# The second mix placed directly behind the first on two other PSUM banks, in a fused convolution and feed-forward block

## The reference, cut to what matters

```python
x = x + conv(layernorm_over_channels(x))
t = tokens(x)                                  # (4, 16384, 48)
t = t + ffn(layernorm_over_channels(t))
return from_tokens(t)

# conv: 3x3 convolution of the first 12 channels, the others pass by
#       1x1 convolution 48 -> 254 channels                          ("mix")
#       in each 8x8 patch: irfft2(rfft2(patch) * fft_w)             ("weigh", "inverse")
#       a, b = halves of 127 channels;  gelu(a) * b                 ("gelu", "gate")
#       1x1 convolution 127 -> 48                                   ("project")
# ffn:  h = relu(quantised(q_mul(x) @ q_mul(W1).T + q_mul(b1)))      48 -> 192
#       y =      quantised(q_mul(h) @ q_mul(W2).T + q_mul(b2))       192 -> 48
```

## Time and profile before

| | |
|---|---|
| median of 3 runs (lowest, highest) | 719.0 us (718.56, 719.1) |
| the profiled execution | 720.83 us |
| its span, first to last instruction | 718.9 us |
| busy share PE, PEld, DVE, ACT, POOL | 93%, 73%, 84%, 75%, 67% |
| mean granted TensorE clock | 0.983 |

### The profile page before, as it was taken

How to read it: one execution, slowest core, us unless ns; L and a number is a source line. 1 busy time by engine, 2 the same in 40 slices (tenths; PEclk the granted TensorE clock), 3 DMA queues, 4 the chain that set the end, 5 groups by cost and what they waited for, 6 DMA issues and landing times.

```text
span 718.9 us, 19183 instructions
## 1 busy us (share of the span) xinstructions
PE 670.5 (93%) x6699; PEld 521.3 (73%) x6699; DVE 600.7 (84%) x1141; ACT 541.3 (75%) x1077; POOL 480.8 (67%) x354
## 2 busy tenths in 40 slices
PE   1579999999999999999999999999999999999973
PEld 1467788777777887778777877778777877777741
DVE  5436789888889898998999999888899899977785
ACT  3144578878888888888888888888888887777774
POOL 2752667877767777877777778777777778753351
PEclk9989999999999999999999999999999999999995
DMA  3342332333434432343334333434433324331111
GB/s 76 90 101 69 85 83 68 88 102 85 106 90 105 103 92 70 100 95 96 101 97 106 98 80 80 106 91 100 94 103 105 102 55 100 87 99 43 29 30 53
DMA packets 46486, 62.22 MB, mean 87 GB/s; under 512 B 19039, under 2 KB 34871, under 8 KB 46391
## 3 DMA queue, kind: packets, MB, share of 16 engines
q1 hardware_dynamic: 45143, 60.91, 33.7%
q10 hardware_dynamic: 1248, 0.08, 0.1%
HBM read 44.62 MB, written 16.35 MB: 85 GB/s over the span
## 4 chain that ended last, share of the span: by engine, by line
PE 76%; DVE 8%; POOL 7%; issue 3%; DMA 2%; ACTq 1%; ACT 1%; SPq 1%; DVEq 0%; POOLq 0%
PE inva L474 15%; PE mixp L461 14%; PE invb L481 14%; PE misc L673 7%; PE misc L490 5%; POOL st L1262 5%; PE misc L545 4%; PE misc L511 4%; PE misc L606 3%; PE misc L658 3%; PE misc L596 2%; PE misc L520 2%; DVE st L1176 2%; DVE qpix L1066 1%; PE misc L568 1%
## 5 line engine op out<-in xcount | busy, mean ns | idle before, releaser
L1009 DVE TENSOR_TENSOR gmix<-mixp,freq_w 128x508 f32<-128x508 f32 x256 | 162.9, 677 | 10.1 <-PE mixp L461 10.1
L474 PE MATMUL inva<-inv,gmix 128*127 128x128 f32 x1024 | 138.8, 279 | 0.2 <-DVE gmix L1009 0.2
L481 PE MATMUL invb<-inv,gmix 128*127 128x128 f32 x1024 | 135.5, 275 | 0.1
L474 PEld LDWEIGHTS inva<-inv,gmix 128*127 128x127 f32 x1024 | 127.0, 192 | 8.6 <-issue 7.8
L461 PE MATMUL mixp<-win,zh 60*128 60x254 f16 x1024 | 120.9, 273 | 5.2 <-DVE gmix L1009 3.5
L481 PEld LDWEIGHTS invb<-inv,gmix 128*127 128x127 f32 x1024 | 124.6, 192 | 0.7 <-DVE hbuf L1020 0.3
L461 PE MATMUL mixp<-win,zl 60*128 60x254 f16 x1024 | 119.6, 269 | 0.0
L1262 POOL TENSOR_TENSOR st<-st,neg_half 128x16 f32<-128x16 f32 x32 | 92.8, 2901 | 36.1 <-DVE st L1185 36.1
L759 ACT ACTIVATE hid<-misc 128x512 f16<-128x512 f32 x186 | 100.9, 599 | 18.2 <-PE misc L545 18.2
L1295 POOL TENSOR_TENSOR st<-st,neg_half 128x16 f32<-128x16 f32 x32 | 98.6, 3080 | 16.8 <-DVE st L1092 16.8
L745 ACT ACTIVATE gact<-inva 127x512 f32<-127x512 f32 x128 | 76.9, 601 | 36.2 <-PE inva L474 36.2
(11 more groups left out here) (122 smaller groups left out, 1223.2 us busy)
## 6 DMA issues: line engine op xcount, KB each, us to landing
xin<-in_x_dram SPq DMA_DIRECT2D x64, 192.0 KB, 3.4
xres<-in_x_dram SPq DMA_DIRECT2D x64, 192.0 KB, 4.2
out_dram<-ob SPq DMA_DIRECT2D x62, 192.0 KB, 2.7
taps<-cz_scratch SPq DMA_DIRECT2D x32, 292.5 KB
crm<-rm_scratch SPq DMA_DIRECT2D x64, 96.0 KB
cz_scratch<-cz SPq DMA_DIRECT2D x64, 48.8 KB
cx<-in_x_dram SPq DMA_DIRECT2D x32, 96.0 KB
rm_scratch<-rm_t SPq DMA_DIRECT2D x120, 4.0 KB
```

The lines of the kernel that those rows point to most:

```text
L474: mm = pe.matmul(inva[0:HID, q * PX:(q + 1) * PX], gmix[:, s % 2, q, 0:HID], inv[:], start=True, stop=True, skip_group_check=True)
L481: mm = pe.matmul(invb[0:HID, q * PX:(q + 1) * PX], gmix[:, s % 2, q, HID:HID2], inv[:], start=True, stop=True, skip_group_check=True)
L1009: dve.tensor_tensor(gmix[:, s % 2, 2 * q:2 * q + 2, 0:HID2], mixp[q][:, 0:2 * HID2].rearrange("p (e c) -> p e c", e=2), freq_w[:], ALU.mul ...
```

## The change

`mix(t, 1)` now writes to `bank[1]` and `bank[2]` and stands directly behind `mix(t, 0)` on PE, ahead of the projection. The projection's second half goes to `bank[0]`, as `bank[2]` is taken, and the second layer uses the `mixp` pair, which weigh 0 must have read. On DVE `weigh(t, 1)` moves from behind `scale_tokens` to directly behind `weigh(t, 0)`, ahead of the two residual additions. Waits are added or exchanged where a bank has a new user. The number of instructions stays the same on each engine, and the order on ACT, POOL and SP is unchanged.

```diff
             def mix(t, s):
-                pe.wait_ge(gmix_ready, upto(8 * n + 2 * s))
+                pe.wait_ge(gmix_ready, upto(8 * n + 2 * (s if s != 1 else 0)))
+                pair = (bank[1], bank[2]) if s == 1 else mixp
...
             def second_layer(t):
-                    pe.wait_ge(xsq_ready, upto(2 * a + 2, 2 * STEPS))
-                    pe.wait_ge(lo_ready, upto(2 * n + 2, 2 * STEPS))
+                pair = mixp
+                pe.wait_ge(gmix_ready, upto(8 * n + 2, 8 * STEPS))
+                pe.wait_ge(y16_ready, upto(2 * l))
...
             def turn_tokens(t):
                 pe.wait_ge(qpix_ready, upto(k + 1))
+                pe.wait_ge(tch_ready, upto(2 * m + 2, 2 * STEPS))
+                pe.wait_ge(gmix_ready, upto(8 * n + 4, 8 * STEPS))
...
-                    pe.wait_ge(y16_ready, upto(2 * l + 2))
...
             def turn_rest(t):
                 pe.wait_ge(tch_ready, upto(2 * m + 2))
+                pe.wait_ge(gmix_ready, upto(8 * n + 4, 8 * STEPS))
...
                     mix(t, 0)
+                    pe.wait_ge(xsq_ready, upto(2 * a + 2, 2 * STEPS))
+                    pe.wait_ge(hid16_ready, upto(6 * l + 6))
+                    mix(t, 1)
                 if live(t, 4):
-                    pe.wait_ge(lo_ready, upto(2 * n + 1, 2 * STEPS))
+                    pe.wait_ge(lo_ready, upto(2 * n + 2, 2 * STEPS))
                     project(t, 0, bank[3])
-                    pe.wait_ge(hid16_ready, upto(6 * l + 6))
-                    project(t, 1, bank[2])
+                    project(t, 1, bank[0])
...
                 if live(t, 3):
-                    mix(t, 1)
                     inverse(t, 3, 0)
...
                 if live(t, 3):
+                    pe.wait_ge(y16_ready, upto(2 * l + 2))
                     mix(t, 2)
...
             def residual(t, half):
-                dve.tensor_tensor(split(dst), split(bank[(3, 2)[half]][:]),
+                dve.tensor_tensor(split(dst), split(bank[(3, 0)[half]][:]),
...
                 if live(t, 3):
                     weigh(t, 0)
+                    weigh(t, 1)
                 if live(t, 4):
                     residual(t, 0)
                     residual(t, 1)
...
                     scale_tokens(t)
-                if live(t, 3):
-                    weigh(t, 1)
```

More of the change, by code:

```diff
@@ L460, in mix @@
                             r0 = HALF * q
-                            mm = pe.matmul(mixp[q][:, e * HID2:(e + 1) * HID2],
+                            mm = pe.matmul(pair[q][:, e * HID2:(e + 1) * HID2],
                                            zpart[r0:r0 + KC, 2 * s + e, :], win[r0:r0 + KC, wpart, :],
@@ L548, in second_layer @@
             def second_layer(t):
[L550 to L556, removed]
-                    pe.wait_ge(xsq_ready, upto(2 * a + 2, 2 * STEPS))
-                    pe.wait_ge(lo_ready, upto(2 * n + 2, 2 * STEPS))
+                n, l = at(t, 3), at(t, 6)
+                pair = mixp
+                pe.wait_ge(gmix_ready, upto(8 * n + 2, 8 * STEPS))
+                pe.wait_ge(y16_ready, upto(2 * l))
                 if late(t, 6):
@@ L582, in turn_tokens @@
             def turn_tokens(t):
-                a, n, k, l = (at(t, d) for d in (0, 3, 5, 6))
+                a, n, m, k, l = (at(t, d) for d in (0, 3, 4, 5, 6))
                 peeled = not FIRST <= t[1] < LAST
                 pe.wait_ge(qpix_ready, upto(k + 1))
+                pe.wait_ge(tch_ready, upto(2 * m + 2, 2 * STEPS))
+                pe.wait_ge(gmix_ready, upto(8 * n + 4, 8 * STEPS))
                 pe.wait_ge(lo_ready, upto(2 * n + 2, 2 * STEPS))
@@ L591, in turn_tokens @@
                     pe.wait_ge(hid16_ready, 6 * LATE + (2 if k > LATE else 0))
-                else:
-                    pe.wait_ge(y16_ready, upto(2 * l + 2))
                 pe.sem_inc(pe_held, 1)
@@ L601, in turn_rest @@
             def turn_rest(t):
-                m = at(t, 4)
+                n, m = at(t, 3), at(t, 4)
                 pe.wait_ge(tch_ready, upto(2 * m + 2))
+                pe.wait_ge(gmix_ready, upto(8 * n + 4, 8 * STEPS))
                 for i in range(PAIRS):
@@ L840, in sums @@
             def sums(t, halves_of):
-                a, l = at(t, 0), at(t, 6)
-                pair = mixp if isinstance(a, int) and a >= TOTAL - 3 else (bank[1], bank[0])
+                l = at(t, 6)
+                pair = mixp
                 act.wait_ge(out_ready, upto(l))
@@ L1009, in weigh @@
                     dve.tensor_tensor(gmix[:, s % 2, 2 * q:2 * q + 2, 0:HID2],
-                                      mixp[q][:, 0:2 * HID2].rearrange("p (e c) -> p e c", e=2),
+                                      pair[q][:, 0:2 * HID2].rearrange("p (e c) -> p e c", e=2),
                                       freq_w[:], ALU.mult).then_inc(gmix_ready, 1)
```

## The result

The changed kernel takes 741.9 us (median of 4 runs, 741.6 to 743.6) against 718.8 us for the kernel before on the same chip: a ratio of 1.033, 95% interval 1.0313 to 1.0346. It is slower by 23 us. The profiled execution has a span of 739.6 us, 20.7 more than before. The difference is less than 23 because the profiled execution of the kernel before, 720.83, was 2 us above its median.

A forecast was written before the change was run, and what follows sets the result against it. PE's work and DVE's chain up to `qpix` were taken to bound the kernel together. 27 x 2.43 = 65.6, minus 6.3, minus 1, gave +58.3 us: 779.1 on the profiled execution, forecast 777, range 744 to 785.

The forecast's parts named there:

- The bound: PE's own work and DVE's chain up to `qpix` end within 0.05 us; delaying `qpix` is paid every step.
- Mix 1 ahead of the projection: On PE, the same matmuls in another order: gain and loss nil in undisturbed steps.
- Weigh 1: On DVE, 1.19 us ahead of `rm`, less 0.79 cover: with DVE alone the step loses 0.40 us.
- `xcen` first by 0.09: POOL's `xcen` starts at 275.25, 0.09 ahead of DVE's `rm` at 275.34, and shuts DVE out.
- POOL doesn't let go between `xcen` and `zpix`: `rm` is shut out until `zpix` ends, so `qpix` starts 2.43 us later in each of 27 steps.
- two signs: The prediction is wrong if `rm` lasts 0.17, or `turn_tokens` starts other than 1.1 behind `qpix`.
- POOL lets both through: Rival: `rm` and `qpix` both run behind `xcen`, 1.32 us a step, net +28, 747; chance 0.10.
- The long steps: Lengthenings from POOL's `cz` work: all 6.3 us given back, bounds 0 and 6.3; the bias meets no `zpix`.
- Steps 3 and 4: Steps without `turn_tokens`, where mix 1's wait partly falls away: 1 us gained for both, bounds 0 and 2.
- the clock falls: Rival: PE's clock drops in its new gap of some 2.4 us a step, +67, 845; chance 0.04.

The follow-up runs named there:

- taking the chain away: Kernel before with only `scale_tokens` moved ahead of `rows` on DVE, so `qpix` precedes `rm`: 711.7 us against 716.4, ratio 0.9942.
- the extra DVE work alone: Kernel before, own banks and PE order, plus two extra DVE additions ahead of the residuals in steps 5 to 31: 746.2 us, ratio 1.038.
- without the shut-out: Changed kernel with POOL waiting for `qpix` before `xcen`, so DVE is always first: 721.6 us, ratio 1.0041 to the kernel before.
- one addition more: Changed kernel with one extra 0.60 us DVE addition ahead of the residuals in steps 5 to 31: 742.1 us, ratio 1.0351.
- the last version: Changed kernel with mix 1 on banks 1 and 0, projection on 3 and 2, DVE order weighings, `qpix`, residuals, `rm`: 706.7 us, ratio 0.9864.
- the kernel with two additions: Changed kernel with two extra DVE additions, 1.19 us, ahead of the residuals: 810.1 us, ratio 1.1285 to the kernel before.
- the bias ahead of `rm`: Changed kernel with the bias moved ahead of `rm` and `qpix` on DVE in steps 6 to 31: 808.4 us, ratio 1.127.

## Why the prediction was wrong

What held, by its steps. *The bound*: PE's work and the chain up to `qpix` end within 0.05 us. The 1.09 to 1.11 from `qpix` to `turn_tokens` and the 9.19 behind it held in the changed kernel, and taking the chain away gave steps of 20.06. *Mix 1 ahead of the projection*: no gain and no loss in the full steps, shown by the extra DVE work alone giving the same step of 21.29. *Weigh 1*: `rm` issued 3.67 behind L1185, predicted 3.66; without the shut-out a step of 20.36, against a predicted 20.11 + 0.40 = 20.51. The 0.15 less is because `rm`, no longer released by a semaphore, is followed by `qpix` after 0.08 rather than 0.21. *`xcen` first by 0.09*: it was, by 0.10, and DVE was shut out.

The step that failed is this one of the prediction: "POOL doesn't let go between `xcen` and `zpix`". I read it from one event, a bias that was issued 0.02 ahead of `zpix`, and applied it to a `rm` that is issued 1.0 ahead of it. In the changed kernel `rm` is let through when `xcen` ends, and `qpix` comes in right behind. The term was sized at 2.43 us a step and measured 1.19 in the step's length (4.68 less 3.47 in the start of `qpix`, 1.21); 27 times the difference of 1.24 is 33, which is most of the 35 us between 777 and 741.9. Neither of the two signs that I had named for being wrong appeared: one looked at whether `rm` is shut out, the other at whether `turn_tokens` hangs on `qpix`, and neither at how long the shut-out lasts. The rival "POOL lets both through" had the right mechanism and 1.32 a step (747), but I gave it 0.10. What the experiments show is what I should have asked for: how long each side had waited. At the end of `xcen`, a DVE instruction issued clearly ahead of `zpix` went first each time: `rm` by 1.0 here, by 0.4 with one addition more, `qpix` by 1.0, the bias by 1.0 and still by 0.06. At the end of that DVE instruction, `zpix` went ahead of an `rm` issued 0.8 or 0.25 behind it. "The one that has waited longer goes first" fits all of these. So does a second rule, that the ports change hands whenever the other engine is already waiting. No experiment parts the two, as each engine issues its next instruction only 0.03 to 0.1 us before the last one ends.

Close races neither rule settles, and there the kind of instruction seems to count. `qpix`, stamped within 0.01 of `zpix`, went first in all 26 steps of the changed kernel that had this race, and in all 27 with one addition more. The bias, also stamped with `zpix` or up to 0.01 ahead, came second in all 26 full steps of the last version, and second in the earlier trace rows with 0.02. The event from which I had read my rule was thus a near tie of a bias, which is lost regularly, and not the case of an `rm` that has waited for 1.0. Why the bias loses near ties and `qpix` wins them is open. The start stamps may not be the moments at which the ports are taken; no run tests that.

*The long steps*: 6.3 us given back, as taken; POOL's output does end earlier before the next step (5.8 us instead of 4.7) and its `cz` work starts about 1 us earlier in it. But the bias still meets `zpix` (1.37 long), which I had ruled out. *Steps 3 and 4*: I took 1 us with bounds 0 and 2; 4.4 were gained ahead of step 5, since mix 1 no longer waits there and the clock stays up. The clock was in my list only as a danger. That is 3.4 us more, and 0.6 came behind step 31. The forecast was thus 37.6 us above the profiled execution's +20.7, and 35 above the median, as the profiled execution of the kernel before was 2 us above its median.

*The rival "the clock falls"* was put at a gap of 2.4 us and had a chance of 0.04. With the gap that the change really makes, 1.18, it didn't come. But had my own 2.43 been right, the gap would have been about 2.4, and the kernel with two additions shows what follows in most steps: 1.5 us more. By its own mechanism the forecast should have been about 777 + 27 x 1.5 = 817 (an estimate from that run), and this rival deserved far more than 0.04.

## What to carry to other kernels

When two engines shut each other out, a move is not priced by its own length: 1.19 us more in front of `rm` cost 1.2 a step, the next 0.60 cost nothing, and the next 0.60 cost 1.1 plus 1.5 for the clock. Two engines that share ports meet there as well as at semaphores, which the description of the cores leaves out. So write down, for both engines, when each instruction that needs the shared ports is issued, and look where the change turns an order round; if the margin is a tenth of a microsecond, put what others wait for in front, or let the other engine wait. And one event in a trace is not a rule: look at how long each side had waited in it before applying it elsewhere.

## What the runs showed of the hardware

DVE and POOL keep each other out for whole instructions also when DVE's is a TENSOR_TENSOR with two inputs in SBUF: `rm` 1.09 instead of 0.17, `qpix` 1.87 instead of 0.95, from an order of 0.10 us. This is what the Trainium skill (SBUF — State Buffer, "Who interferes with whom") says of such instructions; the traces agree. When both waited, the one that had waited clearly longer went next (by 0.06 to 1.0 us); that the ports simply change hands would fit these cases too.

The matrix engine's clock fell behind gaps of 2.29 and 2.47 us in most steps (granted 0.57 over the next 4 us in the steps shown) and didn't behind gaps of 1.18 (granted 1.00). The gap alone doesn't decide it. In the kernel with two additions more, steps 12 and 31 kept 1.00 behind gaps of 2.29 and 2.35, with the bias ahead of `rm` four steps did behind about 2.5, and step 5 of the changed kernel did behind 2.04. In step 3 of the kernel before it fell during the second of two gaps, 1.53 and 1.79, that stood about 1 us apart.
